# Input rows plus graph sums, formed by chunks of five tiles in the key/value part and kept in a table of their own

## What is computed

```python
xn = layernorm(x)
# graph: 4 heads of 64; one neighbour per row; the sum over heads is repeated 4 times
xt = (xn @ weight).reshape(n, 4, 64)
alpha = softmax(leaky_relu(alpha_l[src] + alpha_r[dst]))
tmp = einsum('nh,nhd->nd', alpha[:n], xt[dst[:n]])      # n x 64
graph = tile(tmp, 4)                                    # n x 256
# mix: 8 heads of 64
k, v = instance_norm(k), instance_norm(v)
dots = einsum('bhnd,bhne->bhde', k, v)
mix = (q @ dots / n) @ w_out.T + b_out
x = x + graph + mix
x = x + experts(layernorm(x))                           # top 2 of 6, three layers each
```

## Time and profile before

| | |
|---|---|
| time, median of 3 runs | 752.59 us (751.69 to 754.4) |
| the profiled execution, its own time | 754.05 us |
| its span | 751.9 us |
| busy in the span | PE 670.3, DVE 554.2, ACT 442.1, POOL 448.3 us |
| mean granted TensorE clock | 0.947 |
| DMA | 104.68 MB, mean 139 GB/s |

### The profile page before, as it was taken

One profiled execution on the slowest core, in us unless ns is written; L12 is line 12 of the kernel. 1 busy time (PEld: TensorE's weight loads), 2 busy tenths in 40 slices (PEclk: granted clock), 3 DMA queues, 4 the chain that ended last, 5 costly groups with the idle time before them and its releaser, 6 DMA issues.

```text
span 751.9 us, 15726 instructions
## 1 busy us (share of the span) xinstructions
PE 670.3 (89%) x4705; PEld 619.2 (82%) x4705; DVE 554.2 (74%) x1427; ACT 442.1 (59%) x879; POOL 448.3 (60%) x392
## 2 busy tenths in 40 slices
PE   2987999999999979889875199999999999999993
PEld 2877788888888867867754189999999999999993
DVE  5784679988888876787776257777777777777773
ACT  2655567677777636666773155665656656656651
POOL 3565488876666400425466478888888855555555
PEclk9999999999999999989995579999999999999997
DMA  8887644454443268677744568666546956654443
GB/s 209 199 189 141 153 129 126 141 137 126 128 125 112 72 219 278 187 238 241 220 114 130 138 200 192 125 129 119 113 81 106 177 109 94 95 89 59 50 44 37
DMA packets 90672, 104.68 MB, mean 139 GB/s; under 512 B 27195, under 2 KB 74745, under 8 KB 90593
## 3 DMA queue, kind: packets, MB, share of 16 engines
q1 hardware_dynamic: 58049, 70.98, 33.7%
q0 software_dynamic: 32544, 32.70, 25.3%
HBM read 53.25 MB, written 52.26 MB: 140 GB/s over the span
## 4 chain that ended last, share of the span: by engine, by line
PE 77%; DVE 10%; ACT 3%; DMA 3%; POOL 3%; issue 2%; SPq 1%; POOLq 0%; DVEq 0%; ACTq 0%
PE kv_ps L1361 10%; PE kv_ps L1362 10%; PE kv_ps L1363 10%; PE pt L1353 6%; PE d_ps L1225 6%; PE kv_ps L1202 5%; PE kv_ps L1205 5%; PE kv_ps L1203 5%; PE xt_ps L1353 3%; PE kv_ps L1302 2%; PE pt L1202 2%; PE pt L1205 2%; PE pt L1203 2%; POOL tab L590 1%; DMA al_tab<-arena 1%
## 5 line engine op out<-in xcount | busy, mean ns | idle before, releaser
L1361 PE MATMUL kv_ps<-we_h,now_h 128*128 x648 | 193.5, 299 | 3.7 <-DVE now_l L1172 2.2
L1363 PE MATMUL kv_ps<-we_h,now_l 128*128 x648 | 184.3, 284 | 0.0
L1362 PE MATMUL kv_ps<-we_l,now_h 128*128 x648 | 184.2, 284 | 0.0
L1361 PEld LDWEIGHTS kv_ps<-we_h,now_h 128*128 128x128 f32 x648 | 125.1, 193 | 5.2 <-issue 5.2
L1362 PEld LDWEIGHTS kv_ps<-we_l,now_h 128*128 128x128 f32 x648 | 125.4, 193 | 0.0
L1363 PEld LDWEIGHTS kv_ps<-we_h,now_l 128*128 128x128 f32 x648 | 124.9, 193 | 0.0
L1152 DVE TENSOR_TENSOR work<-kv_ps,be 128x256 f32<-128x256 f32 x216 | 81.7, 419 | 53.3 <-PE kv_ps L1363 53.2
L612 POOL DMA_INDIRECT out_x<-work,arena x56 | 87.6, 1564 | 42.3 <-DVE work L1160 29.5
L792 ACT ACTIVATE now_h<-pt 128x512 fp32r<-128x512 f32 x54 | 32.4, 600 | 106.3 <-PE pt L1353 106.3
L558 POOL DMA_INDIRECT alg<-al_tab,src_all x50 | 62.3, 1246 | 39.0 <-DVE arena L941 14.8
L964 DVE TENSOR_REDUCE ss<-xring 125x16 f32<-125x1040 f32 x50 | 61.6, 1233 | 17.4 <-ACT xring L677 16.2
(11 more groups left out here) (253 smaller groups left out, 1829.2 us busy)
## 6 DMA issues: line engine op xcount, KB each, us to landing
arena<-tab SPq DMA_DIRECT2D x80, 131.0 KB, 2.8
xring<-in_x SPq DMA_DIRECT2D x26, 224.0 KB
we_h<-wt_h SPq DMA_DIRECT2D x6, 768.0 KB, 6.3
we_l<-wt_l SPq DMA_DIRECT2D x6, 768.0 KB, 8.7
xt_tab<-arena SPq DMA_DIRECT2D x7, 568.8 KB
weight_in<-tab SPq DMA_DIRECT2D x28, 131.0 KB, 2.6
out_x<-arena SPq DMA_DIRECT2D x12, 224.0 KB
staged<-in_ew SPq DMA_DIRECT2D x9, 256.0 KB, 5.3
```

The lines of the kernel that those rows point to most:

```text
L1361: pe.matmul(outp, hi[:, c, :], we_h[:, w], start=c == 0, stop=False)
L1362: pe.matmul(outp, hi[:, c, :], we_l[:, w], start=False, stop=False)
L1363: last = pe.matmul(outp, lo[:, c, :], we_h[:, w], start=False, stop=c == KC - 1)
```

## The change

The sum of input rows and graph sums is no longer formed two tiles at a time in the mixing part. It is formed per chunk: SP loads the chunk's input rows into `yc` (the arena's place of `gp`, once `g2` has been made from it), VectorE adds the graph sums in place (`row_sums`), SP stores the result to `y2_tab`, and the next chunk's `gp` waits for that store. `row_sums(m)` stands in tile 5(m + 2) for m up to 7, behind the copies of the dots for m = 8 and in step 2 of the mixing part for m = 9. The mixing part loads rows of `y2_tab` into seven slots, the two new ones where `y2` was, and adds them directly. Lines of the changed kernel lie 29 to 41 further on in the parts of VectorE.

```diff
-SLOTS = 5
+SLOTS = 7
...
+        y2_tab = nc.dram_tensor("y2_tab", (N, D), FP32, kind="Internal").ap()
...
+        yc = arena[0:P, gp_at:gp_at + CH * D].rearrange("p (g n) -> p g n", g=CH)
...
-        y2 = [over(f"y2_{q}", [P, 2 * D], at + 4 * E * F).rearrange("p (l n) -> p l n", l=2)
-              for q, at in enumerate((wkv_h_at, wkv_l_at))]
-        x2in = xring[0:P, :].rearrange("p (s l n) -> p s l n", s=SLOTS, l=2)
+        x2in = [rows.rearrange("p (l n) -> p l n", l=2)
+                for rows in [xring[0:P, 2 * D * s:2 * D * (s + 1)] for s in range(SLOTS - 2)]
+                + [over(f"x2in_{q}", [P, 2 * D], at + 4 * E * F) for q, at in (("h", wkv_h_at), ("l", wkv_l_at))]]
...
+        y2_t = y2_tab.rearrange("(p t) n -> p t n", t=T)
...
-            for r in range(ROUNDS):
-                sp.wait_ge(cvl_done, r + 1)
-                put(r)
-                if r + 2 < ROUNDS:
-                    take(r + 2)
+            def rows_to_sum(m):
+
+                sp.wait_ge(g2_done, m + 1)
+                wide(yc, x_t[:, m * CH:(m + 1) * CH, :], yc_in)
+
+            def sums_out(m):
+
+                sp.wait_ge(yc_done, m + 1)
+                wide(y2_t[:, m * CH:(m + 1) * CH, :], yc, yc_out)
+
+            cv_due = {cv_tile(r): r for r in range(ROUNDS)}
+            for t in range(T):
+                m = t // CH - 1
+                if t % CH == 0 and m >= 1:
+                    sums_out(m - 1)
+                if t % CH == 3 and m >= 0:
+                    rows_to_sum(m)
+                if t - 1 in cv_due:
+                    r = cv_due[t - 1]
+                    sp.wait_ge(cvl_done, r + 1)
+                    put(r)
+                    if r + 2 < ROUNDS:
+                        take(r + 2)
...
             def load_x2(i):
-                wide(x2in[:, i % SLOTS, :, :], x_t[:, 2 * i:2 * i + 2, :], x2_in[i % SLOTS])
+                sp.wait_ge(yc_out, 32 * ((2 * i + 1) // CH + 1))
+                wide(x2in[i % SLOTS], y2_t[:, 2 * i:2 * i + 2, :], x2_in[i % SLOTS])
 
+            sums_out(CHUNKS - 2)
             sp.wait_ge(red_done, T)
-            for i in range(SLOTS):
+            for i in range(SLOTS - 2):
                 load_x2(i)
+            rows_to_sum(CHUNKS - 1)
             sp.wait_ge(dots_done, T)
...
+            for i in range(SLOTS - 2, SLOTS):
+                load_x2(i)
             for i in range(PR):
+                if i == 3:
+                    sums_out(CHUNKS - 1)
                 if i + SLOTS < PR:
-                    sp.wait_ge(y2_done, i + 1)
+                    sp.wait_ge(x2_done, i + 1)
                     load_x2(i + SLOTS)
...
                 if part == 0:
+                    if m >= 1:
+                        dve.wait_ge(yc_out, 32 * m)
                     dve.tensor_tensor(gp, xtg[:, b, :, 0:D].rearrange("p g (h n) -> p g h n", n=GC),
...
+            def row_sums(m):
+
+                dve.wait_ge(yc_in, 32 * (m + 1))
+                dve.wait_ge(gs_done, m + 1)
+                rows = yc.rearrange("p g (h n) -> p g h n", n=GC)
+                dve.tensor_tensor(rows, rows, gsum[:, m * CH:(m + 1) * CH, :].unsqueeze(2).to_broadcast([P, CH, GH, GC]),
+                                  ALU.add).then_inc(yc_done, 1)
...
                     piece(t // CH - 1, t % CH)
+                if t % CH == 0 and t >= 2 * CH:
+                    row_sums(t // CH - 2)
...
+            row_sums(CHUNKS - 2)
             for q in range(2):
                 piece(CHUNKS - 1, q)
...
-            graph_rows(0)
...
-                dve.wait_ge(y2_done, i + 1)
+                dve.wait_ge(x2_in[i % SLOTS], 32 * (i // SLOTS + 1))
                 dve.wait_ge(ma_done, i + 1)
+                if g == 1 and at == 0:
+                    dve.wait_ge(yc_out, 32 * CHUNKS)
...
-                dve.tensor_tensor(xr[g % RB][:, at:at + 2, 0:D], ma_ps[i % 2][0:P, :, :], y2[i % 2],
+                dve.tensor_tensor(xr[g % RB][:, at:at + 2, 0:D], ma_ps[i % 2][0:P, :, :], x2in[i % SLOTS],
...
-                if i + 1 < PR:
-                    graph_rows(i + 1)
+                if i == 2:
+                    row_sums(CHUNKS - 1)
```

More of the change, by code:

```diff
@@ L284, in gps_layer @@
         x2_in = [sem(f"x2_in{s}") for s in range(SLOTS)]
-        ma_done, y2_done, x2_done = sem("ma_done"), sem("y2_done"), sem("x2_done")
+        yc_in, yc_done, yc_out = sem("yc_in"), sem("yc_done"), sem("yc_out")
+        ma_done, x2_done = sem("ma_done"), sem("x2_done")
         bs2_done, ag2_done, sd2_done, fin2_done = sem("bs2_done"), sem("ag2_done"), sem("sd2_done"), sem("fin2_done")
@@ L459, in _ @@
                         sp.dma_start(new[:, e * EW:(e + 1) * EW].bitcast(FP32), tab[e]).then_inc(we_in, 16)
-            sp.wait_ge(y2_done, PR)
+            sp.wait_ge(x2_done, PR)
             sp.dma_start(b3_sb, eb3.rearrange("e n -> (e n)").partition_broadcast(128)).then_inc(b3_in, 16)
@@ L996, in _ @@
                 piece(CHUNKS - 1, q)
-            def graph_rows(i):
-                dve.wait_ge(x2_in[i % SLOTS], 32 * (i // SLOTS + 1))
-                if i == 0:
-                    dve.wait_ge(gs_done, CHUNKS)
-                    dve.wait_ge(v_ready, T)
-                if i >= 2:
-                    dve.wait_ge(x2_done, i - 1)
-                for h in range(2):
-                    last = dve.tensor_tensor(y2[i % 2][:, h, :].rearrange("p (h n) -> p h n", n=GC),
-                                             x2in[:, i % SLOTS, h, :].rearrange("p (h n) -> p h n", n=GC),
-                                             gsum[:, 2 * i + h, :].unsqueeze(1).to_broadcast([P, GH, GC]), ALU.add)
-                last.then_inc(y2_done, 1)
-            graph_rows(0)
             for c in range(KC):
```

## The result

The changed kernel takes **762.38 us** (median of four runs: 754.4, 762.36, 762.41, 762.93), the kernel before on the same chip 752.21 (four runs): a ratio of 1.0101 with a 95% interval of 1.0053 to 1.0149. It is slower by about 1% (the two medians alone, which leave the run of 754.4 out of account, differ by 1.4%). The forecast was no change at 753.7, in a range up to 761.

What follows compares the result with a forecast made beforehand. It took TensorE to set the pace, VectorE having thin slack in the loop. Terms 1.5 + 1.5 - 3.5 + 1.6 = +1.1 us gave 755.2 for the profiled execution, 753.7 against the median; range 748.6 to near 761.

Steps and rivals of the forecast that it cites:

- rival 1: Key/value loop: waits for the new stores or loads bite, 0.5 us in eight chunks, +4 us, 757.7 us; chance 0.24.
- a slow store at the seam: Seam, upper bound: the ninth sum's store lands as slowly as a weight load (7.2 us), given as +4.9 us.
- The price of a chunk's sum: VectorE: each 125x1280 sum costs 1.48 us, taken from the product L941 of the same shape.
- The loop: Key/value loop: eight sums leave VectorE little slack, TensorE doesn't stall, loop ends 1.5 us later; bounds 0 and 5.5.
- The seam: Between loop and mixing part: last product waits for the ninth sum's store, net +1.5 us; lower bound +0.4.
- The mixing steps: Mixing part: five old row sums leave the chain of waits, 0.7 us each, -3.5 us; bounds -2 and -5.
- rival 4: Mixing part: bound by VectorE, so its relief counts in all steps, -10.7 us, 741.9 us; chance 0.03.
- rival 3: Loop and mixing part: last store and loop end on time, larger saving in steps, -4.0 us, 748.6 us; chance 0.22.
- The last store: Step 4: its sum waits 2.9 us for the last chunk's store, 1.3 free, +1.6 us; bounds 0 and +4.
- Rival 2: Seam and step 4: added idle time drops TensorE to half clock for one or two more stretches, 756.2 us; chance 0.13.

Runs made afterwards that it cites:

- run 1: The changed kernel again, no edit: 784.98 us, 1.0096 of the kernel before.
- run 2: Changed kernel with the wait for the last chunk's store moved from step 4 to step 8: 775.7 us, 0.9985 of the kernel before.
- run 5: Kernel before plus eight chunk sums in the loop, on a place nothing reads, without their transfers: 1.0002 of the kernel before.
- run 6: Kernel before plus the eight loads and stores of the change in the loop, without the sums: 0.9996 of the kernel before.
- run 11: Changed kernel with only the two bias loads moved to step 6: 778.31 us, 1.0046 of the kernel before.
- run 12: The changed kernel once more, no edit, on the third chip: 782.23 us, 1.0110 of the kernel before.
- run 9: Kernel before with only the two bias loads moved to step 6: 774.34 us, 1.0000 of the kernel before.
- run 4: Changed kernel with the last store's wait at step 8 and chunk 8 summed in `staged` instead of `yc`: 774.49 us, 0.9960 of the kernel before.
- run 10: run 8 again on the third chip: 770.09 us, 0.9941 of the kernel before.
- run 8: Changed kernel, last two chunks summed elsewhere, step 4 wait removed, biases loaded in step 6, five slot loads ahead of the ninth store: 747.26 us, 0.9944.

## Where the prediction held and where it failed, by its steps

The forecast of no change was wrong by one term, the wait for the last store. The upper end of the range, 761, comes near the measured time by luck: it was made of waits in the loop (rival 1) and a slow store at the seam, and neither came.

**The price of a chunk's sum: right.** Taken from the product as 1.48 us, measured 1482 ns.

**The loop: right in the main, and rival 1 is refuted.** Own pace forecast 18.29 us a chunk; from tile 10 to 15 it is 142.80 - 124.70 = 18.10. Lateness at tile 45 forecast 3.3; it is 251.39 - 247.67 = 3.7 (2.5 in runs 1 and 2, counted from the first key). The last four tiles, forecast at 11.97 us, take 263.29 - 251.39 = 11.90. So the last keys stand 1.9 us later (263.29 against 261.40 in the earlier trace rows), forecast 1.5. The copy of the dots stands 2.8 later, since it waits 0.9 us more for the last eight products (2.24 against 1.32), which take 2.08 us with the clock at 0.70 in that window; in the other profiles with the change the loop is 0.6 to 1.3 us longer. No load or store of the sums is waited for in the loop. That the transfers are free holds for each half alone (runs 5 and 6). Together they cost this 0.6 to 1.3 us, and a gather that lands later at tile 10 may be why; the forecast let POOL's gathers move only with L941.

**The seam: right.** Forecast +1.5, measured +1.6, in the first profile and, at full clock on both sides, in runs 2, 11 and 12 (11.8 against 10.2). (By the working itself the upper bound is 1.5 + 7.2 - 3.4 = +5.3, not +4.9.) The ninth store was issued at 268.64 and let the product start at 272.34, 3.7 us later; the forecast had 3.4 and a little for the second issue. The estimate of 5.9 us that was worked out from the Trainium skill (DMA: Bandwidth & Descriptors, Bandwidth, and Latency and other measured facts) is slower than this measurement, and the measurement decides. The wait was forecast at 1.3 us beyond L994. In the first profile it is 0.8, since TensorE's half clock made L1036 late as well; at full clock it is 1.4, as in run 12:

```profile
268.21 1.49 DVE L972 TENSOR_TENSOR arena<-arena,al 125x1280 f32<-125x1280 f32 x1 [1.38 <-DMA y_tab<-arena]
```

**The mixing steps: right.** Forecast -3.5 (bounds -2 to -5). Against the 116.9 us of runs 5 and 9, whose mixing part is that of before, runs 2 and 4 have -2.7 and -2.1 with the wait gone, runs 10 and 8 with the biases moved -3.9 and -5.2. A closer value can't be given, since the granted clock over these steps differs from profile to profile (0.92 to 0.95). A plain step is still TensorE's: 287.60 - 283.84 = 3.76 us between the sums of steps 4 and 5 in run 2.

```profile
287.60 0.69 DVE L1058 TENSOR_TENSOR arena<-kv_ps,x2in_h 125x512 f32<-125x512 f32 x1 [1.81 <-PE kv_ps L1312]
```

So rival 4 is refuted, and the saving exists. Of rival 3, which wanted a larger saving and no wait for the last store, the second half is refuted.

**The last store: the step that failed.** Mechanism, place and order on SP were as forecast; the size was not. The term was +1.6 (a wait of 2.9, 1.3 of it free; bounds 0 to +4), and it is the difference between steps of 123.17 and of 114.2 us, **+9.0**, the wait being 11.23 (runs 1 and 2, on one chip, differ by 8.6 us in their times and by 11.6 in the steps of their profiles). The forecast took the landing of the weights from the trace of before (7.2 us) and added 1.8 us for the store's bytes, which made 9.0 us from the second weight load's issue to the store's landing. Measured in the changed profile it is 12.4 (from the second weight load at 285.80 to 298.16). Two things were left out, both visible before the run. First, everything that SP issues at the seam shifts against VectorE: the slot loads now stand behind the ninth store, and behind them come the rows of the last chunk (0.64 MB), the biases and two more slots. From 266 to 270 us the DMA share is 0.15, where it was 0.75 before; what should have moved then comes later. VectorE's step 3 is 2.8 us later than before, SP's second weight load 5.1 us (285.80 against 280.68). Second, from 270 us on the DMA engines are full (share 0.90 to 1.08), so the store waits for bytes and not for a landing time. The windows of the changed kernel show how many:

```profile
286.00:290.00 4.00, 4.00 (x30) 3.57 (x28) 0.90 (x6) 2.35 (x6) 0.00 (x0) 1.00 1.08 377
290.00:294.00 4.00, 3.30 (x23) 2.76 (x22) 0.00 (x0) 0.73 (x2) 0.00 (x0) 1.00 1.02 414
294.00:298.00 4.00, 0.00 (x0) 0.00 (x0) 0.00 (x0) 0.00 (x0) 0.00 (x0) 0.97 0.62 239
```

From 286 to 298 us, 4 us x (377 + 414 + 239) GB/s = 4.1 MB move. The store is 0.64 MB of them and the weights at most 1.6; some 2 MB are left, of which one step's load and store, 0.5 MB, were issued behind the store. The rest is a backlog that the forecast took as nothing. The trace's records of single pieces show the order: until about 290 us those of 2 and 1 KB (slots and outputs of earlier steps), from 289 to 294 those of 6 KB (the weights), from 292 to 297 those of 5 KB (the store). The 1.3 us that were taken as free weren't: the sum of step 4 is 9.2 us later than in run 2, counted from the first mixing sum, and nothing of it comes back by step 8.

**Rival 2, the clock: in part.** After the wait the granted clock was 0.50 from 298 to 308 us:

```profile
298.00:308.00 10.00, 7.12 (x30) 6.47 (x30) 3.67 (x14) 3.91 (x9) 0.00 (x0) 0.50 0.75 237
```

In run 2, without the wait, it is 1.00 there:

```profile
298.00:308.00 10.00, 7.62 (x55) 6.46 (x54) 8.10 (x33) 6.69 (x12) 2.42 (x2) 1.00 0.49 147
```

At half speed 7.12 us of TensorE's time do 3.6 us of work. From the sum of step 4 to that of step 8 the changed kernel takes 22.57 us at a mean clock of 0.71, run 2 takes 21.23 at 1.00, so the clock behind the wait costs 1.3 us, and 0.6 to 1.5 us in the other profiles with the wait. From step 8 on the first profile is 1.6 us faster than run 2, so that over all steps nothing of it is left; over the mixing part the mean is 0.88 in both kernels, before and changed. The wait itself, 9.2 us at step 4, is the loss. At the seam half clock added up to 1.5 us in some profiles, with the change and without it (run 5). The trace agrees with the rule of the Trainium skill (TensorE: Matmul & The Clock Gate, HAM oscillation) that products which wait for a transfer start again throttled: the clock is 0.50 behind the 11 us wait.

## What to carry to other kernels

A store issued behind others is priced by the bytes queued ahead of it at that moment, including those that the change itself adds and those that it pushes later; a landing time read from an emptier queue can be far too short (here 9.0 us forecast, 12.4 measured). When a change makes two buffers share a place, look which numbers really overlap: the wait belongs at the first instruction that writes those, and moving it from step 4 to step 8 turned a loss of 1% into no loss. Work can be added to an engine that is nearly the bound if what it feeds is wanted tiles later: 1.48 us more per chunk made the loop of 180 us longer by 0.6 to 1.3 us, and by nothing without the transfers (run 5). But such an engine has little slack left to make up other lateness: 0.27 us a chunk here.

## What the runs showed that was not expected

- The DMA engines can be full at a low rate. In the window from 274 to 278 us of the changed kernel the share is 0.95 at 264 GB/s; from 290 to 294 us, with the weights, 1.02 at 414 GB/s. The records of single pieces show what moves in the first of them: loads of slots in pieces of 2 KB and rows in pieces of 5 KB. The bias loads, issued at 275.53, come in pieces of 6 KB and move from 278 to 284 us (share 0.99 at 359 GB/s from 280 to 284). So what they do to the store comes from their place in the queue and their 1.6 MB, not from a low rate of their own.

```profile
274.00:278.00 4.00, 2.27 (x18) 2.06 (x18) 2.04 (x6) 1.67 (x2) 0.00 (x0) 1.00 0.95 264
```

- The granted clock at the seam fell in some profiled executions and not in others of the same kernel: the window from 262 to 266 us has 0.70 in the changed kernel's first profile and 1.00 in run 12. Why stays open, and so does the single run of 754.4 us (mean clock 0.951, the other three 0.942 to 0.946).
- The chips differ by 3% with the same clock, and not evenly. In the profiles of the kernel before and of run 9 (752 and 771 us spans) TensorE is busy for 184.85 and 184.87 us from 76 to 262 us, but for 70.80 and 64.57 us from 404 to 500, and for 100.00 and 92.56 us from 500 to 600. Matmul by matmul, both kernels stand at 446 to 447 us at the 2200th and 19.3 us apart at the 3200th and at every one behind it; in between 100 of them take 13.3 us or more on the slower chip and 11.7 on the other. So the difference lies in the first part of the experts, from about 450 to 583 us, and nowhere else. What is slower there was not looked into.
